# An attention and mixture-of-experts layer on one core: the front of the kernel reordered, with the k half of the first stack loaded from two queues

## The reference, cut to what matters

```python
x = L0_attn_x                                    # (4, 1024, 128) f32
xn = layernorm(x, eps=1e-5)                      # no gain, no offset
Q = rope(xn @ W_q.T); K = rope(xn @ W_k.T); V = xn @ W_v.T     # 16 heads of 8
attn = softmax(Q @ K.T / sqrt(8)); a = (attn @ V) @ W_o.T
# feed-forward: 8 experts, 2 chosen for each token
w, idx = top_k(xn @ Wg, 2); w = softmax(w)
xhat = (xn - mean) * rsqrt(var + 1e-6)
out_e = relu((xhat * gamma_e + beta_e) @ W1_e + b1_e) @ W2_e + b2_e + xn
return x + a + sum_k w_k * out_{idx_k}
```

## Time and profile before

| what | value |
|---|---|
| median of 3 runs | 664.96 us (664.7 to 665.36) |
| the profiled execution: time | 665.9 us |
| the profiled execution: span, first to last instruction | 664.1 us |
| PE matmul busy | 624.2 us, 94% of the span |
| ACT busy | 508.1 us, 77% |
| DVE busy | 388.1 us, 58% |
| POOL busy | 202.5 us, 30% |
| mean granted TensorE clock | 0.985 of full speed |
| first matmul of the scores | 30.83 us from the start |

### The profile page before, as it was taken

One profiled execution on the slowest core, in us unless ns is written; L12 is line 12 of the kernel. 1 busy time (PEld: TensorE's weight loads), 2 busy tenths in 40 slices (PEclk: granted clock), 3 DMA queues, 4 the chain that ended last, 5 costly groups with the idle time before them and its releaser, 6 DMA issues.

```text
span 664.1 us, 12213 instructions
## 1 busy us (share of the span) xinstructions
PE 624.2 (94%) x4589; PEld 275.0 (41%) x4589; DVE 388.1 (58%) x1150; ACT 508.1 (77%) x551; POOL 202.5 (30%) x243
## 2 busy tenths in 40 slices
PE   3699999999999999999999999999999999999995
PEld 1224422323455555444455555544445555322222
DVE  3975568798555554587755555458775555334112
ACT  2387799888677777777777777777777777999992
POOL 0359200006763433333343343333334331100000
PEclk9979999999999999999999999999999999999997
DMA  6275702003220303100312030310032213451000
GB/s 227 52 190 175 191 1 65 1 0 79 63 60 21 92 26 75 42 17 21 88 52 62 21 92 25 75 42 17 21 88 54 60 17 80 190 188 45 1 1 34
DMA packets 25425, 43.99 MB, mean 66 GB/s; under 512 B 5472, under 2 KB 15248, under 8 KB 24848
## 3 DMA queue, kind: packets, MB, share of 16 engines
q1 hardware_dynamic: 20032, 32.15, 17.7%
q0 software_dynamic: 4608, 9.45, 5.2%
q10 hardware_dynamic: 720, 1.54, 0.6%
HBM read 17.43 MB, written 8.91 MB: 40 GB/s over the span
## 4 chain that ended last, share of the span: by engine, by line
PE 78%; ACT 10%; DVE 7%; issue 2%; DMA 1%; DVEq 1%; SPq 1%; POOL 0%; ACTq 0%
PE acc L527 30%; PE sc L494 18%; PE bank L579 12%; ACT ring L712 10%; PE bank L571 9%; PE bank L564 2%; PE bank L443 2%; PE bank L588 1%; DVE xn L1045 1%; PE bank L433 1%; PE bank L424 1%; DMA const<-shape_constants 1%; PE bank L555 1%; SPq L292 1%; DVEq L1042 1%
## 5 line engine op out<-in xcount | busy, mean ns | idle before, releaser
L712 ACT ACTIVATE ring<-sc 128x1024 f32<-128x1024 f32 x512 | 492.9, 1022 | 126.4 <-PE sc L494 124.9
L527 PE MATMUL acc<-ring,v 128*9 128x512 f32 x2048 | 270.5, 600 | 2.4 <-issue 2.4
L494 PE MATMUL sc<-qs,ks 32*128 32x512 f32 x1024 | 169.6, 500 | 14.2 <-ACT ring L712 9.2
L397 POOL DMA_INDIRECT token_out<-work,token x72 | 79.2, 1100 | 160.8 <-DVE work L1065 155.0
L387 POOL DMA_INDIRECT work<-normed,token x72 | 70.1, 973 | 167.9 <-DVE work L1051 91.8
L494 PEld LDWEIGHTS sc<-qs,ks 32*128 32x128 f32 x1024 | 66.2, 183 | 122.6 <-ACT ring L712 87.3
L579 PEld LDWEIGHTS bank<-xn,work 128*128 128x128 f32 x576 | 69.7, 191 | 65.1 <-issue 29.9
L1058 DVE TENSOR_SCALAR work<-bank,xn 128x128 f32<-128x128 f32 x288 | 80.9, 344 | 23.1 <-PE bank L571 23.1
L579 PE MATMUL bank<-xn,work 128*128 128x128 f32 x576 | 83.2, 287 | 3.1 <-DVE work L1051 3.1
L571 PE MATMUL bank<-work,xn 128*128 128x128 f32 x576 | 77.0, 277 | 1.4 <-DVE norms L779 1.1
L1045 DVE COPY xn<-w_all 128x1158 f32 x72 | 55.8, 776 | 33.2 <-DVE work L1065 32.3
(11 more groups left out here) (158 smaller groups left out, 311.3 us busy)
## 6 DMA issues: line engine op xcount, KB each, us to landing
qs<-hl SPq DMA_DIRECT2D x60, 128.0 KB
ks<-hl SPq DMA_DIRECT2D x60, 128.0 KB
w_all<-L_ffn_W SPq DMA_DIRECT2D x16, 256.0 KB, 4.8
x<-L_attn_x SPq DMA_DIRECT2D x4, 512.0 KB, 7.9
normed<-xn SPq DMA_DIRECT2D x4, 512.0 KB, 5.5
xn<-token_out SPq DMA_DIRECT2D x2, 1024.0 KB, 5.9
w_all<-token_out SPq DMA_DIRECT2D x2, 1024.0 KB, 10.3
out<-x SPq DMA_DIRECT2D x8, 256.0 KB, 2.2
```

Of the source, the lines that this page charges most:

```text
L397: pool.indirect_dma_start(out=y_d[:, :], in_=ys[done % TILE_BUFFERS], in_offset=None, out_offset=bass.IndirectOffsetOnAxis(ap=token[:, 1, ...
L494: last = nc.tensor.matmul(dst, ks[r:r + 32, kb * P:(kb + 1) * P].bitcast(F32R), qs[r:r + 32, at].bitcast(F32R), start=True, stop=not slow)
L527: last = nc.tensor.matmul(acc[qh % 2][32 * j:32 * j + VW, :], v9[:, b, kb, 4 * g + j, :], ring[:, (2 * n + j // 2) % UNITS, j % 2, :], sta ...
L712: nc.scalar.activation(ring[:, (2 * n + u) % UNITS, :, :], sc[u][:, :].rearrange("p (h c) -> p h c", h=2), ACT.Exp, scale=SCALE).then_inc( ...
```

## The change

1. The reciprocal root moves from DVE to POOL: an add of eps and one `pow` with the exponent -0.5 (`rsqrt_of`), for the layer norm of batch 0, of batches 1 to 3, and for xhat. DVE keeps the offsets.
2. PE runs two groups of ten products of `ones` (`warm`), one as soon as `ones` is set, one ahead of the first transposes of xn. Their results are not used.
3. The pieces are projected in the order q first half, k first half, q second half, k second half. The third goes to acc0 and acc1, so that it waits for no piece before it; the fourth goes to sc0. The rotated product comes first and has its own count. DVE turns them in the order 0, 1, 3, 2, and for piece 1 takes the low bits itself (`low_dve`). The bound and the decision come after piece 1, before pieces 3 and 2.
4. SP loads the q half after `low_ok` 1, and two of the four k copies after `low_dve`; ACT issues the other two, ahead of its copies of the values. Then come the k second half (before step 4), the q second half (`later_q_in`, before step 8), the second stack, and `rows`.
5. All four pieces of the values go through bank1 and no longer through acc0 and acc1. The clearing of the two is left out; the first `weigh` waits for `rope_out` 4.

```diff
-ROPE_ORDER = ((0, 0), (0, 1), (1, 1), (1, 0))
+ROPE_ORDER = ((0, 0), (0, 1), (1, 0), (1, 1))
+FRONT_ORDER = (0, 1, 3, 2)
+WARM = (10, 10)
...
+        def load_side(eng, q, cols, landed, s, copies):
+            g = q % 4
+            for c in copies:
+                part = c // 2 if s == 0 else c % 2
+                eng.dma_start(stack[q % 2][s][c:P:COPIES, cols], hl[32 * g:32 * g + 32, s, part, cols]
+                              ).then_inc(landed, 16)
...
+            sp.wait_ge(low_ok, 1)
+            load_side(sp, 0, slice(0, CH), first_in, 0, range(COPIES))
+            sp.wait_ge(low_dve, 1)
+            load_side(sp, 0, slice(0, CH), first_in, 1, range(COPIES // 2))
             sp.wait_ge(low_ok, 2)
-            load_stack(0, slice(0, CH), first_in)
-            sp.wait_ge(low_ok, 4)
-            load_stack(0, slice(CH, S), stack_in[0])
+            load_side(sp, 0, slice(CH, S), stack_in[0], 1, range(COPIES))
+            sp.wait_ge(low_ok, 3)
+            load_side(sp, 0, slice(CH, S), later_q_in, 0, range(COPIES))
             load_stack(1, slice(0, S), stack_in[1])
...
+            def rsqrt_of(src, dst, ts, eps, done):
+                nc.gpsimd.tensor_scalar(small[:, 9, ts], src, eps, None, ALU.add).then_inc(eps_ok, 1)
+                eps_count[0] += 1
+                pool.wait_ge(eps_ok, eps_count[0])
+                nc.gpsimd.tensor_tensor(small[:, dst, ts], small[:, 9, ts], small[:, 10, ts], ALU.pow).then_inc(done, 1)
...
+            def warm(count):
+                for k in range(count):
+                    nc.tensor.matmul(sc[k % 2][:, 0:P], ones[:, :], ones[:, :], start=True, stop=True)
+            pe.wait_ge(ones_ok, 1)
+            warm(WARM[0])
...
+            warm(WARM[1])
             turn(0, 0)
             turn(0, 1)
             pe.wait_ge(wT_ok, 6)
...
+            for r in range(2):
+                project_front(r, sc[r][:, 0:CH], sc[r][:, CH:2 * CH])
+            pe.wait_ge(wvg_ok, 1)
+            project_front(2, acc[0][:, :], acc[1][:, :])
+            pe.wait_ge(rope_out, 1)
+            pe.wait_ge(sq_ok, 1)
+            project_front(3, sc[0][:, 0:CH], sc[0][:, CH:2 * CH])
             pe.wait_ge(head_ok, 1)
             head_norms(0)
-            pe.wait_ge(wvg_ok, 1)
             pe.wait_ge(gate_in, 16)
...
+            values(0, 0)
             check_bound(0)
-            for m in range(2, 4):
...
+            for m in range(1, 4):
+                values(0, m)
+            pe.wait_ge(rope_out, 3)
...
+            act.wait_ge(low_dve, 1)
+            load_side(act, 0, slice(0, CH), first_in, 1, range(COPIES // 2, COPIES))
             for m in range(4):
-                act.wait_ge(v_mm, m + 1)
+                act.wait_ge(bank_full[1], USE["values", 0, m])
...
+            turn_front(0, 0, sc[0][:, 0:CH], sc[0][:, CH:2 * CH])
+            split_high(0).then_inc(high_ok, 1)
+            turn_front(1, 1, sc[1][:, 0:CH], sc[1][:, CH:2 * CH])
+            link(split_high(1))
+            nc.vector.tensor_tensor(hl[:, 1, 1, 0:CH], turned[1][:, :], hl[:, 1, 0, 0:CH], ALU.subtract
+                                    ).then_inc(low_dve, 1)
+            bound(0)
             decide(0)
-            v.wait_ge(v_act, 8)
-            for k in range(2):
-                nc.vector.memset(acc[k][:, :], 0.0).then_inc(acc_clear, 1)
+            v.wait_ge(low_dve, 1)
+            turn_front(2, 3, sc[0][:, 0:CH], sc[0][:, CH:2 * CH])
+            split_high(3).then_inc(high_ok, 1)
+            v.wait_ge(low_ok, 1)
+            turn_front(3, 2, acc[0][:, :], acc[1][:, :])
+            split_high(2).then_inc(high_ok, 1)
             for b in range(1, B):
                 moments(b)
-            factors(slice(TB, T))
+            offsets(slice(TB, T), 2)
```

More of the change, by code:

```diff
@@ L106, in bank_uses @@
     take(0, "bound", 0)
+    for m in range(4):
+        take(1, "values", 0, m)
     for n in range(STEPS):
@@ L371, in _ @@
                                         ALU.mult, ALU.add).then_inc(xn_pool, 1)
+            pool.wait_ge(xh_var, 1)
+            rsqrt_of(small[:, 5, :], 7, slice(0, T), 1e-6, xh_scale)
             pool.wait_ge(xh_scale, 1)
@@ L428, in xnT_is_there @@
                 pe.wait_ge(bank_taken[1 if (b, h) == (0, 1) else 0], USE["turn", b, h])
[L430 to L435, removed]
             def values(b, m):
@@ L439, in values @@
                 enter_bank(1, "values", b, m)
-                values_of(bank[1], b, m).then_inc(bank_full[1], 1)
+                for u in range(2):
+                    t = TB * b + 2 * m + u
+                    last = nc.tensor.matmul(bank[1][:, u * (D + E):(u + 1) * (D + E)], xnT[:, t * P:(t + 1) * P],
+                                            wvg[:, :], start=True, stop=True)
+                last.then_inc(bank_full[1], 1)
             def project_qk(dst, b, c, k):
@@ L697, in _ @@
             nc.scalar.copy(xnT[:, CH:2 * CH], bank[1][:, :]).then_inc(bank_taken[1], 1)
-            for r in range(4):
-                act.wait_ge(proj, r + 1)
-                nc.scalar.activation(square[0][r], sc[r % 2][:, 0:CH], ACT.Square).then_inc(sq_ok, 1)
+            for r, src in enumerate((sc[0], sc[1], acc[0], sc[0])):
+                act.wait_ge(proj, 2 * r + 2)
+                nc.scalar.activation(square[0][r], src[:, 0:CH], ACT.Square).then_inc(sq_ok, 1)
+            act.wait_ge(low_dve, 1)
+            load_side(act, 0, slice(0, CH), first_in, 1, range(COPIES // 2, COPIES))
             for m in range(4):
-                act.wait_ge(v_mm, m + 1)
-                src = acc[m % 2][:, 0:2 * (D + E)].rearrange("p (t c) -> p t c", t=2)
+                act.wait_ge(bank_full[1], USE["values", 0, m])
+                src = bank[1][:, 0:2 * (D + E)].rearrange("p (t c) -> p t c", t=2)
                 nc.scalar.copy(v9[:, 0, 2 * m:2 * m + 2, :, 0:DK],
                                src[:, :, 0:D].rearrange("p t (h d) -> p t h d", h=H)).then_inc(v_act, 1)
-                nc.scalar.copy(score[:, 2 * m:2 * m + 2, :], src[:, :, D:D + E]).then_inc(v_act, 1)
+                nc.scalar.copy(score[:, 2 * m:2 * m + 2, :], src[:, :, D:D + E]).then_inc(bank_taken[1], 1)
             act.wait_ge(table_in, 1)
@@ L738, in _ @@
             nc.vector.tensor_copy(head_of[:, :], head_row).then_inc(head_ok, 1)
[L740 to L744, removed]
-                link(nc.vector.tensor_scalar(y.bitcast(I32), tmp.bitcast(I32), -1.0, float(0x5f3759df), ALU.mult,
-                                             ALU.add))
-                for k in range(3):
-                    link(nc.vector.tensor_tensor(tmp, y, y, ALU.mult))
-                    link(nc.vector.tensor_tensor(tmp, tmp, half, ALU.mult))
-                    last = nc.vector.scalar_tensor_tensor(out=y, in0=tmp, scalar=1.5, in1=y, op0=ALU.add, op1=ALU.mult)
-                    if k == 2 and done is not None:
-                        last.then_inc(done, 1)
-                    else:
-                        link(last)
             def moments(b):
@@ L762, in moments, with offsets @@
                     last = nc.vector.bn_aggr(mv[:, t, :], stats[:, t, :])
-                link(last)
-            def factors(ts):
-                link(nc.vector.tensor_scalar(small[:, 9, ts], mv[:, ts, 1], 1e-5, None, ALU.add))
-                rsqrt(9, 6, ts)
+                last.then_inc(mom_ok, 1)
+            def offsets(ts, done):
+                v.wait_ge(rstd_ok, done)
                 nc.vector.scalar_tensor_tensor(out=small[:, 8, ts], in0=mv[:, ts, 0], scalar=-1.0,
@@ L800, in _ @@
             moments(0)
-            factors(slice(0, TB))
+            offsets(slice(0, TB), 1)
             v.wait_ge(ln_ok, 1)
@@ L890, in tops @@
             def tops(b):
[L891 to L892 removed]
+                v.wait_ge(bank_taken[1], USE["values", b, 3])
                 for t in range(TB * b, TB * (b + 1)):
```

82 lines of the change are left out of this document (37 added, 45 removed).

## The result

The changed kernel takes 662.75 us (median of 17 runs, 661.31 to 663.98) against 664.96 us (17 runs, 663.26 to 666.08): 2.2 us less, ratio 0.9967, 95% interval 0.996 to 0.9974. The direction is the forecast one, the size a third of it (6.6 us were forecast), and the time lies 0.55 us above the range. The profiled execution took 663.26 us with a span of 661.4, against 665.9 and 664.1. One execution of a later experiment, the profiled one of x12 (1783.7 us), ran TensorE far slower throughout: it is in no median here, and of its profile only ACT and DVE are read.

The account below looks back on a forecast made before the run. PE was taken to bound the steps, so the gain comes from the front and first steps: 1.5 + 1.85 + 2.45 = 5.8, +2.6 clock, -1.8 rows, 6.6 us in all; 664.96 becomes 658.4, range 656.3 to 662.2.

Parts of the forecast that it names:

- Reciprocal root: Batch 0's layer norm: POOL's add and pow take 1.0 us in all against DVE's 2.49, saving 1.5.
- my bound of 4.6: High end for the root: pow costing as much as 13 small steps at POOL's pace, 4.6 us.
- Warm-up: Products of ones before xn: transposes 0.75 instead of 1.2, projections 1.73 a pair instead of 3.15; 1.85 us saved.
- A second group at 1.2 GHz, priced at 2.8: Before xn: ten products running at the low clock would end at 13.4 and cost 2.8 us of the saving.
- Order, subtraction, flag, branch: From the projections to the first score: new order and earlier flag save 2.45 us; first score at 25.4.
- I take the clock as kept: First steps: clock stays up, weigh(6) could start 13.8 us after the first exponential; gain 2.6 us.
- rival B: First steps: the clock falls all the same; weigh(6) at 42.7, saving 5.4 us, time 659.6; chance 0.20.
- Rows: Before weigh(6): rows land late, at 40.4, putting weigh(6) at 41.5 and taking 1.8 us off the saving.
- The shift is carried to the end: From step 6 on PE sets the pace, so the 6.6 us saved at weigh(6) lasts to the end.
- POOL's configuration and first use: POOL's first add: it may wait for configuration loading, of which 6.8 us are covered.
- rivals E and F: POOL's first operation waits for configuration: E slower, up to 669.9 us, chance 0.08; F about 665, chance 0.04.
- the estimate of 664.4: At POOL's pow: a second kernel loading of some 6 us on the path would give 664.4 us.

Follow-up runs that it names:

- x12: x11 with batch 0's root as ACT's Sqrt plus a DVE reciprocal, and a second group of 9 products of ones: 660.63 us, ratio 0.9943.
- x10: x5 with a second, unused pow on 8 columns ahead of batch 0's root and a second group of 26 products: 662.08 us, ratio 0.9957.
- x3: The changed kernel with 19 instead of 10 products of ones in the second group: 661.86 us, ratio 0.9953.
- x1: The changed kernel with SP issuing all four k copies and ACT none: 662.54 us, ratio 0.996.
- x2: The changed kernel with batch 0's reciprocal root back on DVE, the later two roots left on POOL: 662.68 us, ratio 0.9968.
- x4: The changed kernel with value pieces 1 and 3 going through sc1 instead of bank1: 661.17 us, ratio 0.9944.
- x5: The changed kernel with a second group of 19 and further products of ones around the value pieces and behind step 0's scores: 659.82 us, ratio 0.9922.
- x11: The changed kernel with values through two homes, warm groups 13 and 17, more products later, rows loaded at 7 us, later root on DVE: 658.17 us.

## Why the prediction was wrong, point by point

*Reciprocal root: mis-sized.* Taken at 1.0 us in all, measured 2.05 (add 0.26, pow 1.68): saving 0.5 instead of 1.5. "The operation is 64 times smaller than the one of 1.27" was the wrong scale: pow goes by 0.16 us a column (1.68, 4.20 and 5.46 us for 8, 24 and 32 columns), 64 times the subtraction's time per element. It lay within my bound of 4.6; I should have priced the middle. x10 shows that this term counts in full.

*Warm-up: the failed step.* "Ten from 7.4 to 10.4, just before xn" had both ends wrong. The products took 0.24 us, not 0.3, and ended at 9.4; xn came at 11.7, not 10.65, by the dear pow. Of the gap of 2.3, forecast as 0.25, the pow is 1.05 and the shorter and earlier products 1.0. Behind it the clock fell, and the first pair of projections cost 3.3 instead of 1.73. The sum for the first group was wrong too, without effect: ten products of 0.6 from 1.0 end at 7.0, not 6.3; they took 4.64 us and ended at 5.7. With the pow this makes turned 0 2.5 us late (17.16 for 14.7), and every later time of the front carries just these 2.5 us: low bits 20.4 for 17.9, flag 24.9 for 22.4, first score 27.9 for 25.4. x3 closed the gap and got 1.1 to 1.3 back. A second group at 1.2 GHz, priced at 2.8, cost nothing where it began so (x1, x2, x4): the clock rose at 10.0 to 10.7, and the group ended ahead of xn.

*Order, subtraction, flag, branch: right.* The differences from turned 0 on are within 0.1 us of the forecast ones: first score 10.75 after it for 10.7. The value round trips ended last as said, 1.3 us each (x4), and the k copies were off the path (x1). One reading in it was wrong, off the path: the 2.08 us to a landing count from the start of an issue (28.06 to 30.14) and were added to its end. The last k copy of changed landed at 25.79, 1.5 us behind the end of its issue and 2.1 ahead of the first score.

*"I take the clock as kept": the second failed step.* It fell in the first steps as in the kernel before; I had rival B at 0.20. Its price of 2.6 us was somewhat too high: x5 and x11 measure 2.2 with the clock kept, since weigh(6) comes 14.2 us after the first exponential (x11), not 13.8. That PE was "about half busy" was seen (3.94 of the 7.5 us up to 29.5, where the clock fell); that the clock could fall after that was left to the rival. The Trainium skill ("TensorE: Matmul & The Clock Gate", section "A second HAM failure mode: psum-queue depth-cycling") had warned of it: its kernel lost the clock under short pauses, and this trace agrees, with no pause over 1.2 us between 22 and 29 and the clock at 0.50 after it.

*Rows: right, but with the clock lost not yet due.* In the changed kernel L577 runs without a wait; with the clock kept (x5) it waits, until 2.1 us after the issue's end, the low end I had given, and x11 is free of it. weigh(6) of x5 at 41.51 is the 41.5 of the prediction; but its first exponential came 1.3 us later than forecast, so that the wait itself cost 0.1 and not 1.8.

*The shift is carried to the end: nearly.* 3.2 became 2.6. The medians differ by 2.2, since the profiled execution of changed lies 0.5 above its median where I had carried over the 0.9 of the kernel before.

*POOL's configuration and first use* (rivals E and F): the add began 0.1 us after the moments and pow took 1.68 then as in x10's second use 1.67. No first-use cost is seen. By the rule of the Trainium skill ("GPSIMD Engine Reference", section "2.1 Instruction dispatch") the first loading would have been over before the add, and this trace agrees; the second one of some 6 us, which the estimate of 664.4 stood on, did not come.

The sum, from its own terms: 6.6 forecast, less 1.0 (pow), less 1.5 (clock at the projections), less 0.9 (clock in the first steps, 2.6, in place of rows, 1.8, which then cost nothing, and 0.1 of the first score) is 3.2, as measured at weigh(6) in this profile. In executions like those of x1 and x2 it is 4.1, with the clock lost in another place. The pow and the clock of the first steps had been priced one at a time, each as a rival with the rest fine. The first two terms hang together in part: the pow made 1.05 of the gap in which the clock fell, but no run here has a cheap pow and ten products, so whether the clock would have held then stays open. The third is its own: x3 closed the gap and lost the clock at 28.6 all the same. Adding all three gives 661.8, within the range and still 0.9 below the measured time.

## What to carry to other kernels

Products of ones are lost if they end too far ahead of the real work (here 2.3 us), and a delay elsewhere (here a dear pow) opens that gap: size them for the moment the data comes, at either clock, and fill the thin stretches too, not only the empty ones. Price several rivals together as well as one by one. A second DMA queue or a faster load is worth nothing until the profile shows that the landing is what ends last.

## What the runs showed of the hardware

The clock's state at a given point differs between executions of the same work: x1, whose program is changed's up to the k copies, has it falling at 7.3 and up at 10.7, x2 up only at 10.6, changed itself up at 5.6 and down at 12.5. The times go with it in part: of the 17 runs of changed, the nine with a mean granted clock of 0.986 or more average 662.3 us, the eight below it 663.1. The spread is 2.7 us over these 17 runs and 0.7 to 0.9 over the 4 or 5 of x5, x10 and x11, whose profiles keep the clock; so few runs show it only roughly. GpSimd's pow costs 0.16 us a column of 128 f32 on top of 0.4. A 64 KB SBUF-to-SBUF copy takes 0.54 to 0.61 us to issue from ACT and about 0.6 from SP, and lands some 2.1 us after the start of the issue. An ACT_TABLE_LOAD took 1.28 us and stood right ahead of the first instruction that needed it, though ACT had been idle before (x12).
